# Decoder layer on one core: layer-norm applies moved from ScalarE to GpSimd as (y - mean) * rstd, and GpSimd's constant-operand copies as tensor-scalar operations

## What is computed

```
x1 = layernorm(x  + linear_attention(x))            # 16 heads, random features exp(q.orf - |q|^2/2), 64 of them
x2 = layernorm(x1 + cross_attention(ctx, x1, ctx))  # per tile, softmax over 128 keys, 16 heads
out = layernorm(x2 + W_down(quant(silu(gate) * up)))  # gate, up = quant(x2) times ternary weights, 1024 wide
layernorm(y) = (y - mean(y)) / sqrt(var(y) + 1e-5)    # over the 256 columns
```

## Time and profile before

| | |
|---|---|
| Median of 3 runs | 572.56 us (571.44 to 573.2) |
| The profiled execution: its span | 572.7 us |
| Busy, share of the span | TensorE 87%, VectorE 83%, ScalarE 82%, GpSimd 68% |
| Instructions on GpSimd | 769 |

### The profile page before, as it was taken

One profiled execution on the slowest core, in us unless ns is written; L12 is line 12 of the kernel. 1 busy time (PEld: TensorE's weight loads), 2 busy tenths in 40 slices (PEclk: granted clock), 3 DMA queues, 4 the chain that ended last, 5 costly groups with the idle time before them and its releaser, 6 DMA issues.

```text
span 572.7 us, 17406 instructions
## 1 busy us (share of the span) xinstructions
PE 498.8 (87%) x5990; PEld 346.3 (60%) x5990; DVE 473.8 (83%) x1380; ACT 468.6 (82%) x843; POOL 387.8 (68%) x769
## 2 busy tenths in 40 slices
PE   3057999999999999999999999999999998977751
PEld 2034777666667666677776777776766666744310
DVE  0783566888989998999999999999999998998671
ACT  0225678999999998999999999999999999987631
POOL 7032665678776777777777777787788876665432
PEclk9995999999999999999999999999999999997775
DMA  5604765656676765656565656665555677353221
GB/s 137 220 0 76 139 121 110 105 119 113 132 129 131 130 118 111 130 118 130 112 127 116 129 114 126 121 125 116 124 121 120 127 122 120 84 113 65 36 48 37
DMA packets 191625, 64.01 MB, mean 112 GB/s; under 512 B 171360, under 2 KB 191328, under 8 KB 191584
## 3 DMA queue, kind: packets, MB, share of 16 engines
q1 hardware_dynamic: 189056, 60.32, 53.5%
q10 hardware_dynamic: 2528, 3.15, 1.7%
HBM read 17.31 MB, written 4.19 MB: 38 GB/s over the span
## 4 chain that ended last, share of the span: by engine, by line
ACT 25%; POOL 21%; PE 20%; issue 11%; DVE 9%; DMA 8%; SPq 4%; ACTq 1%; POOLq 1%; DVEq 0%
DMA hqT<-hq 6%; ACT tT L610 5%; PE bank L1081 4%; POOL pkA L410 4%; POOL hq L465 4%; POOL hq L470 3%; POOL rs L424 3%; ACT pT L616 2%; PE bank L1148 2%; ACT pT L617 2%; SPq L303 2%; ACT x L549 2%; POOL y L414 2%; ACT pkA L505 2%; PE bank L1294 2%
## 5 line engine op out<-in xcount | busy, mean ns | idle before, releaser
L1081 PE MATMUL bank<-wq_hi,xT 128*128 128x512 f16 (+1 forms) x256 | 72.0, 337 | 0.3
L610 ACT ACTIVATE tT<-bank 16x1024 f16<-16x1024 f16 x64 | 65.0, 1016 | 1.2
L460 POOL TENSOR_TENSOR xq<-xm,nmagic 128x256 bf16<-128x256 f32 x32 | 19.6, 614 | 66.4 <-DVE xm L908 66.4
L1148 PEld LDWEIGHTS bank<-kvm,phq 128*128 128x128 f32 x512 | 62.2, 192 | 2.5
L1148 PE MATMUL bank<-kvm,phq 128*128 128x34 f32 x512 | 59.8, 272 | 0.0
L410 POOL TENSOR_TENSOR pkA<-qk,pkA 128x512 f16<-128x512 f32 x32 | 37.5, 1173 | 32.9 <-ACT pkA L505 32.9
L424 POOL TENSOR_TENSOR rs<-ve,mhalf 128x1 f32<-128x1 f32 x96 | 52.8, 550 | 0.0
L1294 PE MATMUL bank<-downT,hqT 128*128 128x256 bf16 x256 | 34.6, 280 | 16.5 <-DMA hqT<-hq 16.4
L862 DVE TENSOR_REDUCE negm<-bank 128x4 f16<-128x512 f32 x64 | 43.8, 684 | 5.5 <-PE bank L1197 5.1
L1241 PE MATMUL bank<-pT,ctxv 128*32 128x128 f32 x1024 | 41.6, 281 | 6.8 <-ACT pT L617 6.7
L912 DVE SCALAR_TENSOR_TENSOR g<-th,bank 128x512 f32<-128x512 f32 x64 | 43.3, 676 | 4.0 <-ACT th L640 3.8
(11 more groups left out here) (180 smaller groups left out, 1637.3 us busy)
## 6 DMA issues: line engine op xcount, KB each, us to landing
xs<-in_x_dram SPq DMA_DIRECT2D x32, 128.0 KB, 2.7
xr<-in_x_dram SPq DMA_DIRECT2D x32, 128.0 KB, 2.5
cs<-in_ctx_dram SPq DMA_DIRECT2D x32, 128.0 KB, 2.6
out_dram<-ot SPq DMA_DIRECT2D x32, 128.0 KB, 2.1
ffn_ld<-in_L_ffn_w_gate_dram ACTq DMA_DIRECT2D x1, 1024.0 KB, 5.8
ffn_ld<-in_L_ffn_w_up_dram ACTq DMA_DIRECT2D x1, 1024.0 KB, 8.7
ffn_ld<-in_L_ffn_w_down_dram ACTq DMA_DIRECT2D x1, 1024.0 KB, 10.6
pkAT<-pkA SPq DMA_TRANSPOSE x64, 3.3
```

The costliest lines, as they stand in the source:

```text
L610: last = sc.activation(tT[p + 32:p + 48, :, :], at_mT.bitcast(F16)[p + 32:p + 48, :].unsqueeze(1).to_broadcast([DK, PAIRS, P]), ACT.Copy)
L1081: last = T.matmul(o, xT[:, 2 * part + c, :], w[:, c, cols], start=(n == 0), stop=(n == 5))
L1148: last = T.matmul(at_num[:, 2 * DV * k:2 * DV * (k + 1)], phq[:, par, k, :], kvm[:, k, :, :].rearrange("p h d -> p (h d)"), start=False, s ...
```

## The change

The three applies leave ScalarE. On GpSimd each becomes one tensor-scalar operation with two per-partition operands, (y + nm) * rs, and the `nmr` products go. Each apply follows its `rs` step or, for `x1`, `ya2`. The `rs` steps now also wait for the apply of the tile before. The copies `xhi`, `chi`, `xqf`, `hq0`, `hq1` become tensor-scalar operations with two immediates, instead of tensor-tensor ones with a broadcast constant. Several waits of GpSimd go through `wait_ahead`, which computes the counts before it waits and can now wait for transfers too.

```diff
-                wait(pool, f"nm{n}", t)
-                wait(pool, f"pw{n}", t)
-                g.tensor_tensor(nmr[n - 1][:, :], nm[n - 1][:, :], rs[n - 1][:, :], ALU.mult).then_inc(
-                    done[f"rs{n}"], 1)
+
+            def layernorm_apply(n, par, o, name):
+
+                g.tensor_scalar(o, y[n - 1][:, par, :], nm[n - 1][:, :], rs[n - 1][:, :], ALU.add,
+                                ALU.mult).then_inc(done[name], 1)
...
+            def x1_(t, par):
+                wait_ahead(pool, t, ("pw1", 0), ("nm1", 0), ("ya2", -2))
+                layernorm_apply(1, par, x1[:, par, :], "x1")
...
             def rs2(t, par):
                 wait(pool, "y2", t)
+                wait(pool, "x2", t, -1)
                 rstd(2, t, par)
+
+            def x2_(t, par):
+                wait_ahead(pool, t, ("pw2", 0), ("nm2", 0), ("ad3", -2))
+                layernorm_apply(2, par, x2[:, par, :], "x2")
...
+            def ot_(t, par):
+                earlier = t * 8 - par * 8
+                wait_ahead(pool, t, ("pw3", 0), ("nm3", 0), queues=((stored[par], earlier),))
+                layernorm_apply(3, par, ot[:, par, :], "ot")
...
-                landed(pool, x_in, t, par)
-                wait(pool, "xTp", t, -1)
-                g.tensor_tensor(xpk[:, 0, :], xs[:, par, :], onesf[:, 0:1].to_broadcast([P, D]),
-                                ALU.mult).then_inc(done["xhi"], 1)
+                wait_ahead(pool, t, ("xTp", -1), queues=((x_in[par], t * 8 - par * 8 + 16),))
+                g.tensor_scalar(xpk[:, 0, :], xs[:, par, :], 1.0, 0.0, ALU.mult, ALU.add).then_inc(done["xhi"], 1)
...
-                wait(pool, "hm0", t)
-                g.tensor_tensor(hq[:, 0, :], hm[:, 0, :], nmagic[:, :].to_broadcast([P, 512]),
-                                ALU.add).then_inc(done["hq0"], 1)
+                wait_ahead(pool, t, ("hm0", 0))
+                g.tensor_scalar(hq[:, 0, :], hm[:, 0, :], 1.0, -MAGIC, ALU.mult, ALU.add).then_inc(done["hq0"], 1)
...
             def iteration(i, par):
                 go(xqf, i, par, 8)
@@ -477,8 +489,11 @@
                 go(hq0, i, par, 9)
                 go(rs1, i, par, 5)
                 go(ya2, i, par, 7)
+                go(x1_, i, par, 5)
                 go(rs3, i, par, 10)
+                go(ot_, i, par, 10)
                 go(rs2, i, par, 7)
+                go(x2_, i, par, 7)
                 go(xhi, i, par, 0)
                 go(xlo, i, par, 0)
                 go(xb_, i, par, 4)
...
-            def layernorm_apply(n, par, o, name):
-                sc.activation(o, y[n - 1][:, par, :], ACT.Identity, bias=nmr[n - 1][:, :],
-                              scale=rs[n - 1][:, :]).then_inc(done[name], 1)
...
-                go(x1_, i, par, 5)
...
-                go(ot_, i, par, 10)
-                go(x2_, i, par, 7)
```

More of the change, by code:

```diff
@@ L56, in decoder_kernel @@
         lneps = sb("lneps", [P, 1])
-        nmagic = sb("nmagic", [P, 1])
         mhalf = sb("mhalf", [P, 1])
@@ L160, in decoder_kernel @@
         nm = [sb(f"nm{n}", [P, 1]) for n in "123"]
-        nmr = [sb(f"nmr{n}", [P, 1]) for n in "123"]
         pb = [bank(f"bank{i}") for i in range(8)]
@@ L238, in wait, with wait_ahead @@
                 eng.wait_ge(done[name], v)
-        def wait_ahead(eng, t, *producers):
+        def wait_ahead(eng, t, *producers, queues=()):
             counts = [t + off + 1 for _, off in producers]
             counts = [v if isinstance(v, int) else eng.to_reg(v) for v in counts]
+            bytes_in = [v if isinstance(v, int) else eng.to_reg(v) for _, v in queues]
             eng.wait_ge(ids, 3)
+            for (semaphore, _), v in zip(queues, bytes_in):
+                if not isinstance(v, int) or v > 0:
+                    eng.wait_ge(semaphore, v)
             for (name, _), v in zip(producers, counts):
@@ L361, in _ @@
             g.memset(lneps[:, :], LN_EPS).then_inc(zeroed, 1)
-            g.memset(nmagic[:, :], -MAGIC).then_inc(zeroed, 1)
             g.memset(pkA[:, :, :, :], 0.0).then_inc(zeroed, 1)
@@ L365, in _ @@
             g.memset(vv[:, :, :, :], 0.0).then_inc(zeroed, 1)
-            pool.wait_ge(zeroed, 18)
+            pool.wait_ge(zeroed, 17)
             for m in (idf, idh, idb):
@@ L424, in rstd @@
                 g.tensor_tensor(rs[n - 1][:, :], ve[n - 1][:, :], mhalf[:, :], ALU.pow).then_inc(done[f"pw{n}"], 1)
-                wait(pool, f"nm{n}", t)
-                wait(pool, f"pw{n}", t)
-                g.tensor_tensor(nmr[n - 1][:, :], nm[n - 1][:, :], rs[n - 1][:, :], ALU.mult).then_inc(
-                    done[f"rs{n}"], 1)
+            def layernorm_apply(n, par, o, name):
+                g.tensor_scalar(o, y[n - 1][:, par, :], nm[n - 1][:, :], rs[n - 1][:, :], ALU.add,
+                                ALU.mult).then_inc(done[name], 1)
             def rs1(t, par):
                 wait(pool, "y1", t)
+                wait(pool, "x1", t, -1)
                 rstd(1, t, par)
+            def x1_(t, par):
+                wait_ahead(pool, t, ("pw1", 0), ("nm1", 0), ("ya2", -2))
+                layernorm_apply(1, par, x1[:, par, :], "x1")
             def rs2(t, par):
                 wait(pool, "y2", t)
+                wait(pool, "x2", t, -1)
                 rstd(2, t, par)
+            def x2_(t, par):
+                wait_ahead(pool, t, ("pw2", 0), ("nm2", 0), ("ad3", -2))
+                layernorm_apply(2, par, x2[:, par, :], "x2")
             def rs3(t, par):
@@ L441, in rs3 @@
                 rstd(3, t, par)
+            def ot_(t, par):
+                earlier = t * 8 - par * 8
+                wait_ahead(pool, t, ("pw3", 0), ("nm3", 0), queues=((stored[par], earlier),))
+                layernorm_apply(3, par, ot[:, par, :], "ot")
             def chi(t, par):
-                landed(pool, c_in, t, par)
-                wait_moved(pool, "cT", t, par, -1)
+                before = (par - 1) % 2
+                wait_ahead(pool, t, queues=((c_in[par], t * 8 - par * 8 + 16),
+                                            (moved["cT"][before], (t - 1 - before) * 8 + 16)))
                 c3 = cs[:, par, :].rearrange("p (h d) -> p h d", h=H)
-                g.tensor_tensor(pkC[:, :, 0:2, :], c3.unsqueeze(2).to_broadcast([P, H, 2, DK]),
-                                onesf[:, 0:1].unsqueeze(2).unsqueeze(3).to_broadcast([P, H, 2, DK]),
-                                ALU.mult).then_inc(done["chi"], 1)
+                g.tensor_scalar(pkC[:, :, 0:2, :], c3.unsqueeze(2).to_broadcast([P, H, 2, DK]), 1.0, 0.0,
+                                ALU.mult, ALU.add).then_inc(done["chi"], 1)
             def clo(t, par):
@@ L457, in xqf @@
             def xqf(t, par):
-                wait(pool, "qnt", t)
-                g.tensor_tensor(xq[:, par, :], xm[:, par, :], nmagic[:, :].to_broadcast([P, D]),
-                                ALU.add).then_inc(done["xqf"], 1)
+                wait_ahead(pool, t, ("qnt", 0))
+                g.tensor_scalar(xq[:, par, :], xm[:, par, :], 1.0, -MAGIC, ALU.mult, ALU.add).then_inc(done["xqf"], 1)
             def hq0(t, par):
-                wait(pool, "hm0", t)
-                g.tensor_tensor(hq[:, 0, :], hm[:, 0, :], nmagic[:, :].to_broadcast([P, 512]),
-                                ALU.add).then_inc(done["hq0"], 1)
+                wait_ahead(pool, t, ("hm0", 0))
+                g.tensor_scalar(hq[:, 0, :], hm[:, 0, :], 1.0, -MAGIC, ALU.mult, ALU.add).then_inc(done["hq0"], 1)
             def hq1(t, par):
-                wait(pool, "hm1", t)
-                g.tensor_tensor(hq[:, 1, :], hm[:, 1, :], nmagic[:, :].to_broadcast([P, 512]),
-                                ALU.add).then_inc(done["hq1"], 1)
+                wait_ahead(pool, t, ("hm1", 0))
+                g.tensor_scalar(hq[:, 1, :], hm[:, 1, :], 1.0, -MAGIC, ALU.mult, ALU.add).then_inc(done["hq1"], 1)
             def iteration(i, par):
```

## The result

The changed kernel takes 646.69 us (median of 4 runs, 640.27 to 649.61) against 572.07 us before: ratio 1.128, 95% interval 1.123 to 1.132. The forecast had the sign and the place, and 597 us; its range ended at 613. The span of the profiled execution is 647.6 us.

The account below looks back on a forecast made before the run. It took a GpSimd-ScalarE chain of waits, 14.83 us per tile with PE close behind, as the bound. 572.7 + 28.5 (22 periods at 16.3 us) - 4 (filling and emptying) = 597 us, range 580 to 613.

Parts of the forecast that it names:

- What bounds the kernel: From 240 to 470 us: a per-tile chain of waits of 14.83 us through GpSimd and ScalarE, with PE close behind.
- what the cut loop gives: Cutting the GpSimd-ScalarE chain of waits at x1 gives back 0 to 0.4 us per tile before PE itself binds.
- What is moved: GpSimd's x2 apply waits about 2.5 us for `ad3`, delaying `xlo`, `xb` and `nf`: period 16.3 us where 14.83 stands.
- The prices: New GpSimd operations: 0.45 us for a 256-column copy, 0.78 for 512 columns, 0.50 for an apply.
- loop A: Through PE from `xTp` to `kvp`, then `kvm`, `ad3`, x2 apply, `xhi`, `xlo` and `xTp` again: 16.24 us.
- Filling and emptying: Outside the 22 periods, cheaper applies and copies save 3 us in emptying and 1 in filling; at most 6 in all.
- Only the cut loop counts: Rival: `xlo` is over before PE wants it, PE runs at its own pace: faster, 558 us; chance 0.07.
- GpSimd and VectorE blocking one another: Rival: VectorE's `nlo` or `xm` is hit in each tile, up to +0.43 us, 606 us; chance 0.09.
- Waits that add up: Rival: PE's and VectorE's lateness feed each other, 17.2 us per tile, +20 us more, 617 us; chance 0.06.

Follow-up runs that it names:

- x2 behind `xb`: The changed kernel with GpSimd's x2 apply moved from ahead of `xhi` to behind `xb`, nothing else: 562.46 us, ratio 0.980 to the kernel before.
- The copies alone: The kernel before with the five copies as tensor-scalar operations and their waits as in the change, applies still on ScalarE: 567.15 us, ratio 0.987.
- the applies alone: The changed kernel with the x2 apply after `xb` and all five copies put back to the two-operand form: 573.92 us, ratio 1.000.

## Why the prediction was wrong in size

- **What bounds the kernel; what the cut loop gives.** Right: PE was close behind, with 0 to 0.4 us a tile to give back; it gave 0.13.
- **What is moved.** Right in each place: the wait for `ad3` (2.45 us, 2.5 forecast), `xTp` late by 1.73 to 1.81 us (1.8), VectorE waiting for `xb` and `nf`, tiles at full clock 16.45 us apart (16.3). The chain there is a third loop that I had not written down. It runs from `xTp` through PE up to `qkm`, and on VectorE from `qk` to `ad3`; the chain of waits from 328 to 346 us has it, 16.45 us from apply to apply. `nf` "near 356.4" is 356.53 by its own terms, which changes nothing.

```profile
328.99 0.07 POOL x L427
...
330.81 0.39 PE bank L1064 x4
...
337.69 0.69 DVE qk L764
...
344.85 0.40 DVE y L965
...
345.45 0.08 POOL x L427
```

- **The prices.** On the loop, an apply cost 0.52 us where 0.50 was taken and `xhi` 0.44 where 0.45 was; `chi` was cheaper, 0.62 for 0.78. The period of 16.45 in place of 16.3 adds 3 us over 22. The sum also starts from a span, 572.7, as if it were a run's time; each span profiled since is some 2 us below the time of its execution (647.6 and 649.61).
- **The step that failed** is the one that says that PE "gets slack" and that the period of 16.3 us holds in all 22 tiles. It takes loop A's 13.69 us on PE at a clock of 1.00, which had been read in a stretch where PE was never idle for long. The stall that this same step finds is itself what lowers the clock: 43 us of the 75. No term stood for it and no rival either. A sign of it was in the trace of before, in the emptying (shown below): after two stretches of 5 us with PE busy 3.56 and 3.04 us, the granted clock is 0.58 from 515 to 520 us. The range would have had to reach 22 x (21.0 - 15.0) = +132 us, a long fall in every tile. The Trainium skill ("TensorE: Matmul & The Clock Gate", Part 1) describes a clock gate that goes to half rate after idleness, at 1.2 GHz. The trace agrees in the level (the same two matmuls at 1.28 and 0.73 us), and I had not drawn on it; but the idle gap that the page warns of is longer than any of the stalls ahead of `xTp` here, and the measurement decides.

```profile
505.00:510.00 5.00, 3.56 (x35) 2.11 (x30) 4.86 (x12) 3.42 (x7) 3.89 (x15) 1.00 0.66 134
510.00:515.00 5.00, 3.04 (x48) 2.19 (x50) 4.44 (x16) 4.96 (x10) 2.75 (x5) 1.00 0.30 61
515.00:520.00 5.00, 4.65 (x45) 2.40 (x46) 4.13 (x13) 2.56 (x6) 4.54 (x11) 0.58 0.64 101
```

- **Filling and emptying.** -4 was forecast, +0.4 found. In the runs in which the clock holds from tile to tile it is -3 to -8, the -8 with x2 behind `xb`: its span of 559.3 less 324.65 for the 22 periods is 234.65, against 242.6. The copies alone gave 3.4 us there, the applies alone 3.5.
- **Rivals.** Only the cut loop counts: no, but it is what the moved line gives (-2%). GpSimd and VectorE blocking one another: `nlo` takes 0.310 us in the mean and 0.547 at most, where before it took 0.406 and 0.732; it is hit less than before, not more. Waits that add up: at full clock, no.

What stays open: why the clock falls in about every second tile rather than in each. The idle times ahead of a fall and ahead of none are alike (1.73 and 1.81 us).

## What to carry to other kernels

When an in-order engine takes over a step, look first at what the step waits for and at who stands behind it in the new queue; the same operations cost +13% or gained 2% by the place of one line. When a stall is put into TensorE, price the clock too, with the lower level for the matmuls that follow, and take that price into the range. Relieving one engine is worth little where another is nearly as full: here ScalarE's busy time fell by 8%, and the tile got 0.13 us shorter.

## What the runs showed of the hardware

A stall of PE in each tile of some 16 us brought its clock to the lower level, and the more often the longer it was: in 3 of 22 tiles with 0.85 us, 8 with 1.4, 11 with 1.7 to 1.8, and in all 22 with 2.0. In the changed kernel a fall lasted some 7 or 10 us and made the tile 3 or 4.6 us longer. Filling the idle time with unused matmuls won 39 us.

On GpSimd a tensor-scalar copy takes 0.42 to 0.44 us for 256 columns and 0.62 us for 512, where the two-operand form takes 0.61 to 0.65 and 1.04. So 256 more columns cost 0.2 us, 0.7 to 0.8 ns each, on top of some 0.2 us that do not depend on the columns. The slope bears out what the Trainium skill says of one-input operations ("GPSIMD Engine Reference", Engine selection: "roughly line-rate"); an estimate from the rate alone is too low, 0.43 us for the 512 columns that took 0.62.
